# Reordering four engines around the start of a fused FFN: GpSimd's attention pieces of one step, ScalarE's W*Y split, and one attention product behind the first gate and up

## The reference, cut to what matters

```
x1  = x  + tanh(g_xattn) * attention(layernorm(x), ctx)
x2  = layernorm(x1)
out = x1 + tanh(g_ffn) * ffn(x2)

attention:  Q, K, V = x @ Wh, ctx @ Wh, ctx @ Wh      (4 heads of 128)
            masked  = (Q K^T) * decay
            A       = maximum(abs(masked summed over all 64 sequences), 1)
            O       = A @ V
            Y       = normalised O * gamma + beta
            W       = relu(layernorm(x) @ wg)
            result  = (W * Y) @ wo
ffn:        h = silu(x2 @ gate.T * gate_s) * (x2 @ up.T * up_s)     (1408 wide)
            result = h @ down.T * down_s
```

## Time and profile before

| | |
|---|---|
| median of 3 runs | 1550.93 us (1549.24 to 1554.6) |
| the profiled execution | 1549.4 us, its span 1547.4 us |
| busy | PE 1503.5 us (97%), DVE 1056.2 (68%), POOL 726.3 (47%), ACT 683.0 (44%) |
| chain that ended last | PE 80%, POOL 6%, ACT 5%, DVE 5% |
| mean granted TensorE clock | 0.995 of full speed |

### The profile page before, as it was taken

The page is one execution under the profiler, slowest core; times in us unless marked ns, Lnnn a source line. Parts: engine busy times, 40 slices in busy tenths (PEclk is TensorE's granted clock), DMA queues, the critical chain, the costliest instruction groups (busy, mean ns, idle before and its releaser), DMA issues.

```text
span 1547.4 us, 20330 instructions
## 1 busy us (share of the span) xinstructions
PE 1503.5 (97%) x7226; PEld 1257.7 (81%) x7226; DVE 1056.2 (68%) x1497; ACT 683.0 (44%) x1067; POOL 726.3 (47%) x775
## 2 busy tenths in 40 slices
PE   6999999999799989999999999999999999999998
PEld 5888888887688878888888778888788888888887
DVE  7677778786567656677665766652777877778772
ACT  4444444445454535445453554533344444444442
POOL 4556666762344534445352553524226337237235
PEclk9999999999899999999999999999999999999999
DMA  7888879865668767887677786677174383472322
GB/s 232 275 259 274 266 265 295 263 224 181 225 186 233 203 171 223 213 244 222 195 233 192 198 234 183 197 215 203 62 218 133 107 226 106 124 220 96 122 111 83
DMA packets 374598, 305.93 MB, mean 198 GB/s; under 512 B 258336, under 2 KB 284320, under 8 KB 374304
## 3 DMA queue, kind: packets, MB, share of 16 engines
q1 hardware_dynamic: 374496, 304.61, 65.6%
HBM read 200.23 MB, written 117.31 MB: 205 GB/s over the span
## 4 chain that ended last, share of the span: by engine, by line
PE 80%; POOL 6%; ACT 5%; DVE 5%; issue 2%; DMA 2%; SPq 1%; ACTq 0%; DVEq 0%; POOLq 0%
PE ps L1648 33%; PE pyb L1546 13%; PE po L1648 8%; PE ptb L1648 5%; PE pyb L1648 5%; PE ptb L1546 5%; PE ps L1581 5%; PE po L1546 4%; POOL wyt L1434 2%; ACT turned L666 1%; PE ptb L1551 1%; POOL reg L1471 1%; ACT xn L696 1%; POOL rs L1386 1%; POOL reg L1430 1%
## 5 line engine op out<-in xcount | busy, mean ns | idle before, releaser
L1383 POOL TENSOR_SCALAR rs<-mv 128x1 f32<-128x1 f32 (+1 forms) x132 | 57.6, 436 | 310.8 <-DVE mv L1032 154.5
L1471 POOL TENSOR_TENSOR reg<-tmp,reg 128x512 fp32r<-128x512 f32 x88 | 124.1, 1410 | 128.1 <-ACT reg L717 128.1
L1546 PE MATMUL pyb<-reg,xreg 128*128 128x512 f32 x720 | 178.7, 397 | 0.7 <-DVE xreg L945 0.7
L1648 PE MATMUL ps<-reg,gate 128*128 128x512 f32 x704 | 176.0, 392 | 1.7 <-DVE tmp L1165 1.7
L1648 PE MATMUL ps<-reg,up 128*128 128x512 f32 x704 | 173.9, 389 | 0.0
L1648 PE MATMUL ps<-op,wbuf 128*128 128x512 f32 x704 | 173.9, 389 | 0.0
L1648 PE MATMUL ps<-xreg,reg 128*128 128x512 f32 x704 | 164.2, 391 | 7.2 <-POOL reg L1471 5.9
L1648 PEld LDWEIGHTS ps<-xreg,reg 128*128 128x128 f32 x704 | 131.6, 188 | 35.5 <-POOL reg L1471 6.8
L1455 POOL TENSOR_TENSOR p5b<-p5b,p1b 128x512 f32<-128x512 f32 x44 | 57.0, 1294 | 218.1 <-ACT p5b L741 218.1
L1648 PEld LDWEIGHTS ps<-reg,gate 128*128 128x128 f32 x704 | 131.8, 190 | 28.6 <-issue 2.1
L1648 PEld LDWEIGHTS ps<-reg,up 128*128 128x128 f32 x704 | 132.2, 188 | 27.5
(11 more groups left out here) (147 smaller groups left out, 2804.1 us busy)
## 6 DMA issues: line engine op xcount, KB each, us to landing
wbuf<-ws_scratch SPq DMA_DIRECT2D x44, 896.0 KB, 4.9
xr<-in_x SPq DMA_DIRECT2D x63, 512.0 KB, 5.5
raw<-in_ctx_t SPq DMA_DIRECT2D x32, 512.0 KB, 4.7
w_scratch<-tmp SPq DMA_DIRECT2D x64, 256.0 KB, 4.9
v_scratch<-tmp SPq DMA_DIRECT2D x64, 256.0 KB, 4.0
raw<-v_scratch SPq DMA_DIRECT2D x32, 512.0 KB, 6.0
x_scratch<-xr SPq DMA_DIRECT2D x32, 512.0 KB, 4.5
xr<-x_scratch SPq DMA_DIRECT2D x32, 512.0 KB, 6.3
```

What stands on the lines that cost most here:

```text
L1383: e.tensor_scalar(dst, var, eps, None, ALU.add).then_inc(s["eps"])
L1471: e.tensor_tensor(hid[1][:, m % 11, :], tmp[:, m % 3, :], f(hid[0][:, m % 11, :]), ALU.subtract).then_inc(s["hlo"])
L1546: last = e.matmul(dst, lhs[a], rhs[b], start=(k == 0 and i == 0), stop=(k == n - 1 and i == 2))
L1648: last = e.matmul(dst, l, r, start=(k == 0 and i == 0), stop=(k == n - 1 and i == 1), skip_group_check=sums)
```

## The change

No instruction is added or taken away, and no transfer moves on SP. On four engines instructions change places:

1. PE: `o(2)` goes ahead of `x2_t(2)`, and `o(3)`, the O of the fourth pair, goes behind the first gate and up.
2. DVE, opening: `y_stats(4)` goes ahead of `x2_lo(2)`, and `y_stats(5)` ahead of `v_lo(3)`, which is now behind `x2_lo(3)`.
3. ACT: in the opening `x2_hi(3)` goes ahead of `v_hi(3)`. In the steps `wy_pair_hi` comes first and `norm2_pair` last.
4. POOL: the attention pieces of step 10 of a group go behind the group's last `hidden_lo`, which stands in step 11. Step 10 has such pieces in three groups alone: the second (`wy_pair_lo(8)` and `y_rstd_pair(10)`), the fourth (`rstd2_pair(16)`) and the sixth (`wy_pair_lo(25)` and `y_rstd_pair(27)`).

```diff
@@ ScalarE
             x2_hi(0)
             x2_hi(1)
             x2_hi(2)
+            x2_hi(3)
             v_hi(3)
-            x2_hi(3)
@@
                     for q, piece in pieces(15 * g + step):
+                        if piece == 7:
+                            wy_pair_hi(q)
+                    for q, piece in pieces(15 * g + step):
                         if piece == 0 and q + 1 < B // 2:
                             v_hi(q + 1)
                         if piece == 1:
...
                         if piece == 6:
                             y_pair_affine(q)
-                        if piece == 7:
-                            wy_pair_hi(q)
+                    for q, piece in pieces(15 * g + step):
                         if piece == 10:
                             norm2_pair(q)
@@ VectorE
             norm2(3)
+            y_stats(4)
             x2_lo(2)
+            x2_lo(3)
+            y_stats(5)
             v_lo(3)
-            x2_lo(3)
...
-            y_stats(4)
-            y_stats(5)
@@ GpSimd
+            def attention(n):
+                for q, piece in pieces(n):
+                    if piece == 0:
+                        y_rstd_pair(q)
+                    if piece == 7:
+                        wy_pair_lo(q)
+                    if piece == 9:
+                        rstd2_pair(q)
...
                     if 1 <= step <= 11:
                         hidden_lo(11 * g + step - 1)
-                    for q, piece in pieces(15 * g + step):
-                        if piece == 0:
-                            y_rstd_pair(q)
-                        if piece == 7:
-                            wy_pair_lo(q)
-                        if piece == 9:
-                            rstd2_pair(q)
+                    if step == 11:
+                        attention(15 * g + 10)
+                    if step != 10:
+                        attention(15 * g + step)
@@ TensorE
                         for q, piece in pieces(15 * g + step):
-                            if piece == 0:
+                            if piece == 0 and q > 3:
                                 o(q)
...
                         if step < 11:
                             up_mm(exact, g, step)
+                            if g == 0 and step == 0:
+                                o(3)
...
+            o(2)
             x2_t(2)
-            o(2)
             x2_t(3)
```

## The result

The changed kernel takes 1547.97 us (median of 12 runs, 1544.78 to 1550.32), the kernel before 1551.54 beside it (12 runs, 1548.52 to 1554.60). The ratio is 0.9975, 95% interval 0.9967 to 0.9984: 2.5 to 5.1 us faster where 10.6 was forecast. The prediction's time (1540.4) and its range (to 1546.5) are both missed. The time of 1548 lies 1 us above the third rival's 1546.9, and the ratio does not fit that rival's "no change" quite either.

What follows compares the result with a forecast made beforehand. PE, busy 97% of the span, was taken as the bound, through its waits and clock. 4.3 + 3.0 + 0.3 + 1.5 + 1.5 = 10.6 us gained gave 1540.4 us; range of 8 in 10: 1535 to 1546.5.

Steps and rivals of the forecast that it cites:

- third rival: Opening and step 10: both waits only change their name, 4.0 us gain left, 1546.9 us, no change; chance 0.13.
- the opening keeps 4.3: Opening: second gate 7.7 us earlier, less a new wait of 3.4 us at `wo_mm(4)`, leaves 4.3 us.
- first rival: Opening: the transfers don't hold pair 2 back, PE keeps all 7.7 us, 1537.0 us; chance 0.17.
- so the 16 of gate and up take 3.8, to 395.9: Opening, TensorE: the first gate and up, 16 matmuls from about 392.1, take 3.8 us and end at 395.9.
- from below: Opening's lower bound: if PE's lower clock follows the wait at `wo_mm(4)`, 1.65 us more goes and 2.6 is left.
- second rival: Opening's gaps and `wo_mm(4)`: the clock falls in the new gaps, 2.85 us lost, 1543.3 us; chance 0.15.
- 3.0 gained: Second group's step 10: 3.95 + 1.65 saved, less a new 2.6 us wait for `wy_pair_lo(8)`; between 2.7 and 4.0.
- the wait of 3.95 with its 1.65 of clock is gone: Second group's step 10: `hidden_lo` done at 549.4, so PE's 3.95 us wait and 1.65 us clock loss vanish.
- which covers the nine waits of 0.17: 1.5: Even pairs: `wy_pair_hi` ahead of `norm2` brings the low part up to 1.5 us earlier, gaining 1.5 us.
- "1.5" at 858.66: PE's 3.01 us wait at 858.66: without `norm2` ahead the low part comes 1.5 us earlier, gaining 1.5 us.
- I cost it at nothing: ScalarE in the steps: `norm2` late by up to 2.1 us, with x2's transposes and DRAM trip, costs PE nothing.
- fourth rival: 14 even pairs: late `norm2` reaches PE through `x2_pair_lo`, 1.3 us each, +18.2 - 10.6, slower at 1558.5 us; chance 0.05.

Runs made afterwards that it cites:

- E1: The kernel before with the opening's edits alone (TensorE, VectorE and ScalarE), steps of the groups as they were: 1550.89 us, ratio 1.0003.
- E2: The kernel before with GpSimd's edit of step 10 alone: 1550.61 us, ratio 0.9996.
- E3: The kernel before with ScalarE's order in the steps alone: 1546.87 us, ratio 0.9975.
- E7: E6 with the down weights issued ahead of `v_load(4)` on SyncE: 1529.78 us, ratio 0.9857.
- E9: E6 without the opening's edits, and with the down weights issued ahead of `v_load(4)`: 1535.53 us, ratio 0.9895.
- E11: The changed kernel with nothing but the down weights issued ahead of `v_load(4)`: 1543.12 us, ratio 0.9941.
- E4: The changed kernel with `norm2_pair` back ahead of `v_hi`, `y_normal` and the affine, still behind `wy_pair_hi`: 1541.08 us, ratio 0.9944.
- E10: E7 with `o(2)` back behind `x2_t(2)` on PE: 1530.10 us, ratio 0.9865.
- E5: E4 with GpSimd's step 10 as in the kernel before: 1540.47 us, ratio 0.9933.
- E6: E4 with `wy_pair_lo` left in step 10 and only `y_rstd_pair`, `rstd2_pair` behind the last `hidden_lo`: 1535.44 us, ratio 0.9900.

## Why the prediction was wrong, by its own steps

Its three parts, and what each measured alone against the kernel before:

| part | forecast gain, us | alone, us | 95% interval |
|---|---|---|---|
| opening (E1) | 4.3 | -0.5 | -2.2 to 1.1 |
| step 10 (E2) | 3.0 + 0.3 | 0.6 | -1.2 to 2.3 |
| ScalarE (E3) | 1.5 + 1.5 | 3.9 | 2.3 to 5.4 |
| all (the change) | 10.6 | 3.9 | 2.5 to 5.1 |

(Ratios times 1551.) The parts add up; the two moves of waits failed, and the third came near in size by luck: gains that were sized too small or not seen, and a cost put at nothing, cancel.

**The opening, "the opening keeps 4.3".** Right: no 7 us wait, the first gate at 392, the queue of SyncE as the thing that holds pair 2 back, and its size as a wait (2.1 at pair 2, 0.7 at pair 3, 0.2 at the gate at 412: 3.0, forecast 3.4). E7, E9 and E11 show that cause: 5 to 6 us come back when the transfers are moved, so the first rival, that they do not hold pair 2 back, is out. Wrong: the clock. The step "so the 16 of gate and up take 3.8, to 395.9" took the clock as 1.00 there; they took 5.8 (392.07 to 397.89), while `o(3)` behind them took the 1.6 foreseen. The clock was at its lower level over the first gate in each of the eight profiled executions with the new order (the changed kernel's, E1, E4 to E7, E10, E11), so the second gate was 6.3 earlier (399.32 for 405.60), not 7.7. And the 1.65 that "from below" was to go behind the wait at pair 2 went in four of five such executions (E1, E4, E5 and E6, not in that of the changed kernel). 7.7 - 1.4 - 3.0 - 1.7 = 1.6 against 1.0 in E1's trace. So the second rival, given 0.15, was the likelier course. It struck in both gaps, at 1.4 and 1.7, which together is near the single loss of 2.85 at which it was priced.

**Step 10, "3.0 gained".** The new wait was 2.45 for a forecast 2.6, and VectorE did go first. The step that failed is "the wait of 3.95 with its 1.65 of clock is gone": the clock also fell behind the wait of 2.45, in three of four executions (the changed kernel, E2, E11; not E4). I had taken 3.01 with the clock at 1.00 for a sign that waits below it are free, one execution's row. E1 and E2 have the lower level behind just that wait (3.04 and 3.01 us there; the windows 857.2 to 860.6 and 855.6 to 859.1 are at 0.50). What is left is 1.5, as 3.95 - 2.45; the sixth group added between -0.6 and 0.7. And both edits are not independent: E3 shows the second group's wait at 1.59 already without edit 4, so the sum counted some of it twice. E6 shows what the place can give.

**ScalarE, "which covers the nine waits of 0.17: 1.5" and "1.5" at 858.66.** The second is right (3.01 to 1.39, and E3 1.43). The first was right and mis-sized: each wait costs about 0.47, not 0.17, about 4.2 in all. "I cost it at nothing", of the late `norm2`, is the step that failed outright. The fourth rival named the step and the victim, and was wrong in its pairs and its path: not the transfer of x2 or `x2_pair_lo` delays PE, but the transposes that stand ahead of the W*Y product on DVE. The price is the odd pairs' 3.1, pair 31's 1.8 and pair 25's 1.6, 6.5 in all by the traces, and 6.9 by the medians or 4.8 by the ratios (E4). I had looked for slack in what consumes `norm2` and not in what is queued behind its consumer.

The chances: 0.82 for faster by over 0.3% was too much. The ratio's interval, 0.16% to 0.33% faster, lies mostly within 0.3%. The third rival had the right size for a half-right reason: the opening and step 10 did give nearly everything back, but the 1 us that it left to the opening cannot be told in E1, and what remains is all ScalarE's.

**Open:** why a wait shown as 0.17 costs 0.32 before the first matmul (no record shows the other 0.15); which execution has the lower clock behind a given wait; and 1.0 to 3.1 us that PE waits at 836 to 852, in all kernels, for VectorE to take a `down_mm` result out of its bank (line 1165 of before), which no run here touched.

## What to carry to other kernels

When an instruction is moved back on one engine, follow the queue of each engine that waits for it: what stands behind the waiting instruction is late too, and if it shares a port with a third engine it can lose its turn (the product's 2.29 for 1.23). Two edits can each measure nothing and be worth 6 us together when a second wait stands right behind the first, so after an edit that removed its wait without a gain, look for the wait that replaced it and remove that one as well before dropping the edit. Do not read "the clock stays up behind waits of this size" from one row: in these traces the same wait of 2.45 us had either level behind it.

## What the runs showed of the hardware that was not expected

A VectorE operation with two SBUF inputs and one of GpSimd delay each other by which starts first, and the difference can be 0.1 us: the product took 1.23 us when 0.56 ahead of `hidden_lo` and 2.29 when 0.08 behind it. That is the exclusive port of which the Trainium skill speaks ("SBUF — State Buffer", SBUF: two separate sides), and the trace agrees with it. GpSimd's small ones pay as well: its `TENSOR_SCALAR` of 128x2 took 0.22 free and 1.19 beside VectorE's subtraction (`rs<-mv` at 547.77 in E3 and at 550.24 in the changed kernel).

PE's clock fell behind waits far shorter than the 7 us of before: behind 2.39 and 1.40 with 0.7 to 1.1 of work between, behind 1.06 and 1.40 (E10), and behind single waits of 2.1 to 2.5 us in seven of ten cases, for 3.4 us or about twice that. Length alone does not decide it. The waits of 1.94 at 842.9 in E6 and at 845.1 in E11 had the lower level behind them; those of 2.55 and 2.54 in the sixth group (the changed kernel, E11) and of 3.08 at 847.9 in E3 had not. The spread over the runs of one kernel, up to 6 us, is of the size of a few such falls of 1.7 us; that they are its cause is not shown.
